# A two-layer language-model tower on one core: four-bit rounding in one step fewer, an output bias added by GpSimd, two small products in different row halves

## The reference, cut to what matters

```python
def step(state, inp):                     # the recurrence, 128 steps, all sequences at once
    d_t, p_t = inp
    state = silu(d_t + state) + p_t
    return (state, state)
h = h + (states @ out_w.T + out_b)        # out_w: (256, 64), out_b: (256,)

def fp4_quant_dequant(x):                 # blocks of 16 along the last dimension
    scale = maximum(max(abs(xb)) / 6.0, 1e-12)
    xn = xb / scale
    idx = searchsorted(_MID, abs(xn))     # nearest of 0, .5, 1, 1.5, 2, 3, 4, 6; ties go down
    return _GRID[idx] * sign(xn) * scale

gate, y = fp4_linear(x, w_gate), fp4_linear(x, w_up)     # 256 -> 704 each
return fp4_linear(silu(gate) * y, w_down)                # 704 -> 256
```

## Time and profile before

| | us |
|---|---|
| median of three runs | 592.85 |
| profiled execution | 593.54 |
| its span, first to last instruction | 591.5 |
| PE busy | 526.8 (89%) |
| DVE busy | 447.4 (76%) |
| ACT busy | 247.7 (42%) |
| POOL busy | 203.6 (34%) |
| mean granted clock of TensorE | 0.958 of full |

### The profile page before, as it was taken

The page is one execution under the profiler, slowest core; times in us unless marked ns, Lnnn a source line. Parts: engine busy times, 40 slices in busy tenths (PEclk is TensorE's granted clock), DMA queues, the critical chain, the costliest instruction groups (busy, mean ns, idle before and its releaser), DMA issues.

```text
span 591.5 us, 9139 instructions
## 1 busy us (share of the span) xinstructions
PE 526.8 (89%) x2919; PEld 317.7 (54%) x2934; DVE 447.4 (76%) x1122; ACT 247.7 (42%) x765; POOL 203.6 (34%) x421
## 2 busy tenths in 40 slices
PE   2789989989999999999998997984569999999994
PEld 1566557456556556555555644632236555565663
DVE  1254788898798789789789787485679998988863
ACT  1174255146246236226317417413345555454431
POOL 6402243233323123113113203120346766775311
PEclk9999999999999999999999998995579999999997
DMA  6800000000000000000000000004200000000000
GB/s 183 277 11 11 9 1 21 9 0 9 18 0 9 9 0 0 0 1 0 0 0 0 0 0 2 1 1 84 58 2 9 20 9 18 10 19 11 18 19 18
DMA packets 13518, 12.76 MB, mean 22 GB/s; under 512 B 2795, under 2 KB 12724, under 8 KB 13492
## 3 DMA queue, kind: packets, MB, share of 16 engines
q1 hardware_dynamic: 12212, 10.34, 6.6%
q0 software_dynamic: 1280, 2.11, 1.3%
HBM read 8.25 MB, written 2.10 MB: 17 GB/s over the span
## 4 chain that ended last, share of the span: by engine, by line
PE 54%; DVE 12%; issue 10%; POOL 9%; ACT 8%; SPq 4%; DMA 2%; DVEq 0%; POOLq 0%; ACTq 0%
PE psum L673 19%; PE psum L627 5%; SPq L392 4%; PE psum L640 3%; DVE neg_max L1350 3%; POOL u_now L528 3%; POOL hq L509 3%; PE psum L755 3%; PE psum L775 3%; PE psum L591 3%; PE psum L739 3%; ACT probs L1036 2%; PE psum L948 2%; PE psum L978 2%; PE psum L964 2%
## 5 line engine op out<-in xcount | busy, mean ns | idle before, releaser
L673 PE MATMUL psum<-expw_sb,n2T 128*128 128x512 f32 x256 | 116.5, 597 | 0.0
L446 POOL TENSOR_TENSOR rstd<-meanvar,ln_eps_col 128x1 f32<-128x1 f32 x64 | 12.7, 199 | 257.4 <-DVE meanvar L1331 257.2
L948 PE MATMUL psum<-wguT,n2T 128*128 128x512 f32 (+1 forms) x192 | 81.7, 576 | 0.0
L1036 ACT ACTIVATE probs<-psum,neg_max 128x128 f32<-128x128 f32 x256 | 69.1, 418 | 27.7 <-DVE neg_max L1350 27.7
L673 PEld LDWEIGHTS psum<-expw_sb,n2T 128*128 128x128 f32 x256 | 46.2, 190 | 45.9 <-issue 45.9
L1004 ACT ACTIVATE probsT<-psum 128x512 f32<-128x512 f32 (+2 forms) x88 | 39.6, 463 | 49.4 <-PE psum L627 30.7
L948 PEld LDWEIGHTS psum<-wguT,n2T 128*128 128x128 f32 x192 | 37.7, 198 | 38.8 <-issue 33.6
L978 PE MATMUL psum<-wdT,probsT 128*128 128x256 f32 x192 | 49.8, 402 | 0.1
L1416 DVE SCALAR_TENSOR_TENSOR acc<-psum,g_w,acc 128x256 f32<-128x256 f32 x96 | 42.1, 479 | 7.5 <-PE psum L673 3.1
L1183 ACT ACTIVATE probs<-u_now 64x16 f32<-64x16 f32 x128 | 27.4, 214 | 47.4 <-POOL u_now L528 31.8
L1350 DVE TENSOR_REDUCE neg_max<-psum 128x4 f32<-128x512 f32 x64 | 40.3, 679 | 6.0 <-PE psum L617 3.8
(11 more groups left out here) (172 smaller groups left out, 980.2 us busy)
## 6 DMA issues: line engine op xcount, KB each, us to landing
expw_sb<-in_expert_w SPq DMA_DIRECT2D x8, 256.0 KB
expw_sb<-hidden SPq DMA_DIRECT2D x16, 128.0 KB
result<-res SPq DMA_DIRECT2D x16, 128.0 KB
w_raw<-in_w_down SPq DMA_DIRECT2D x1, 704.0 KB, 9.1
w_raw<-in_w_gate SPq DMA_DIRECT2D x1, 640.0 KB, 7.2
w_raw<-in_w_up SPq DMA_DIRECT2D x1, 640.0 KB, 7.6
wexp_sb<-in_w_expand SPq DMA_DIRECT2D x1, 256.0 KB, 3.2
wproj_sb<-in_w_project SPq DMA_DIRECT2D x1, 256.0 KB, 3.3
```

Of the source, the lines that this page charges most:

```text
L673: last = mm(pq[:, g, :], n2T[:, u, k, :], expw_sb[:, k, EPQ * g:EPQ * (g + 1), :].rearrange("p e n -> p (e n)"), start=(k == 0), stop=(k = ...
L948: last = mm(pgu[u][:, c0:c1], xqT[:, u, k, :], wguT[:, k, c0:c1], start=(k == 0), stop=(k == KD - 1))
L1036: last = nc.scalar.activation(probs[:, u, h, :], pq[:, g, j * T:(j + 1) * T], ACT.Exp, bias=neg_max[:, u, h:h + 1])
```

## The change

Three edits in one.

**Rounding.** The multiplication of the scale (step 2) goes. The reciprocal is taken of the scale itself, and step 4 becomes one operation with two multiplications, by a factor just under 1 and by the reciprocal. The steps are renumbered: 2 reciprocal, 3 values, 4 ScalarE's sizes, 5 and 6 the rounding. The same is done for the weights (nine steps in place of ten). In DVE's queue step 5 of tile `j + 3` of x (before: step 6 of tile `j + 2`, behind `h_fp4(2, j)`) now stands behind `result(j - 1)`, just ahead of `h_product(j + 1)`.

```diff
                 elif k == 2:
-                    V.tensor_scalar(sc[:, 0, :], sc[:, 1, :], -TIE_DOWN, None, ALU.mult).then_inc(steps[2], 1)
+                    V.reciprocal(sc[:, 0, :], sc[:, 1, :]).then_inc(steps[2], 1)
                 elif k == 3:
-                    V.reciprocal(sc[:, 2, :], sc[:, 0, :]).then_inc(steps[3], 1)
-                elif k == 4:
-                    V.tensor_tensor(t3, s3, per_block(2), ALU.mult).then_inc(steps[4], 1)
+                    V.scalar_tensor_tensor(out=t3, in0=s3, scalar=-TIE_DOWN, in1=per_block(0), op0=ALU.mult,
+                                           op1=ALU.mult).then_inc(steps[3], 1)
...
                 h_fp4(0, j)
                 h_fp4(1, j)
+                if j == 0:
+                    x_fp4(5, j + 2)
                 h_fp4(2, j)
                 if second:
                     x_fp4(6, j + 2)
                 h_fp4(3, j)
-                if second:
-                    x_fp4(7, j + 2)
-                h_fp4(4, j)
                 if third:
                     x_fp4(0, j + 3)
                     x_fp4(1, j + 3)
                     x_fp4(2, j + 3)
                     x_fp4(3, j + 3)
-                    x_fp4(4, j + 3)
                 if fourth:
                     add_outp(j + 4)
+                h_fp4(5, j)
                 h_fp4(6, j)
-                h_fp4(7, j)
...
                 if j > 0:
                     result(j - 1)
+                if third:
+                    x_fp4(5, j + 3)
                 h_product(j + 1, FIRST if j + 2 == TILES else WHOLE)
             j = TILES - 1
-            for k in range(5):
+            for k in range(4):
                 h_fp4(k, j, FIRST)
             h_product(j, SECOND)
             h_fp4(0, j, SECOND)
+            h_fp4(5, j, FIRST)
             h_fp4(6, j, FIRST)
-            h_fp4(7, j, FIRST)
-            for k in range(1, 5):
+            for k in range(1, 4):
                 h_fp4(k, j, SECOND)
             result(j - 1)
+            h_fp4(5, j, SECOND)
             h_fp4(6, j, SECOND)
-            h_fp4(7, j, SECOND)
             result(j)
```

```diff
+            def out_bias(s0, s1):
+                pool.wait_ge(a_rest, 16 * (len(a_loads) - ATTENTION_LOADS))
+                pool.wait_ge(ln_norm[2], s1)
+                pool.tensor_tensor(hidden[:, s0:s1, :], hidden[:, s0:s1, :],
+                                   outb_sb[:].unsqueeze(1).to_broadcast([T, s1 - s0, D]),
+                                   ALU.add).then_inc(out_biased, s1 - s0)
...
                 if rec:
                     rstd_of(2, 1, before)
                     convolved(i, 1, 0, 2)
+                    out_bias(2 * i - 2, 2 * i)
                 gather_amid(i)
...
                     if not front:
                         convolved(i, 0, 0, 1)
                         rstd_of(2, 1, n[1])
+                        out_bias(2 * i, 2 * i + 1)
+                        out_bias(2 * i + 1, 2 * i + 2)
...
-            sp.wait_ge(h3_done, SEQS)
+            sp.wait_ge(out_biased, SEQS)
```

**Row halves.** The last chunk of the 704 rows is taken as the 128 columns 576 to 703, all transposed; the product uses partitions 64 to 127 of it (rows 640 to 703). `outp` uses partitions 0 to 63.

```diff
+HIDDEN_CHUNKS = [(128 * k, 0) for k in range(KI - 1)] + [(INNER - 128, 64)]
...
-                    last = mm(pdown, hqT[0:rows, u, k, :], wdT[0:rows, k, :],
-                              start=(k == 0), stop=(k == KI - 1))
+                    last = mm(pdown, hqT[row:, u, k, :], wdT[row:, k, :], start=(k == 0), stop=(k == KI - 1))
```

More of the change, by code:

```diff
@@ L65 @@
 WEIGHT_PIECES = 6
-WEIGHT_STEPS = 10
+WEIGHT_STEPS = 9
 GU_JOBS = (GU_TILES + 1) // 2
@@ L256, in tower @@
         mix_step = sems("mix_step", 2)
-        h3_done = sem("h3_done")
+        h3_done, out_biased = sem("h3_done"), sem("out_biased")
         xn3T_done, n3T_ready = sem("xn3T_done"), sem("n3T_ready")
@@ L957, in h_transposed @@
                 u, start = j % 2, first_chunks(j)
-                pe.wait_ge(qh[8], j + 1)
-                for k in range(KI):
-                    rows = min(128, INNER - 128 * k)
+                pe.wait_ge(qh[7], j + 1)
+                for k, (c0, _) in enumerate(HIDDEN_CHUNKS):
                     if k == start and j == TILES - 1:
-                        pe.wait_ge(qh[8], j + 2)
+                        pe.wait_ge(qh[7], j + 2)
                     at = k * 128 if k < start else 512 + (k - start) * 128
-                    last = nc.tensor.transpose(pgu[u][0:rows, at:at + 128], hq[:, u, k * 128:k * 128 + rows], ident[:])
+                    last = nc.tensor.transpose(pgu[u][:, at:at + 128], hq[:, u, c0:c0 + 128], ident[:])
                     if k == start - 1:
@@ L971, in down @@
                 wait(pe, res_ready, j)
-                for k in range(KI):
-                    rows = min(128, INNER - 128 * k)
+                for k, (_, row) in enumerate(HIDDEN_CHUNKS):
                     if k == 0:
@@ L1189, in sizes @@
             def sizes(values, dst, steps, n):
-                act.wait_ge(steps[4], n)
-                nc.scalar.activation(dst, values, ACT.Abs, scale=MAGIC).then_inc(steps[5], 1)
+                act.wait_ge(steps[3], n)
+                nc.scalar.activation(dst, values, ACT.Abs, scale=MAGIC).then_inc(steps[4], 1)
             def x_sizes(j):
@@ L1207, in h_transposed @@
                 u = j % 2
-                start, rows = first_chunks(j), INNER - 128 * (KI - 1)
+                start, (_, row) = first_chunks(j), HIDDEN_CHUNKS[KI - 1]
                 act.wait_ge(hqT_done[0], j + 1)
@@ L1215, in h_transposed @@
                 at = 512 + (KI - 1 - start) * 128
-                copy(hqT[0:rows, u, KI - 1, :], pgu[u][0:rows, at:at + 128], hqT_ready[1])
+                copy(hqT[row:, u, KI - 1, :], pgu[u][row:, at:at + 128], hqT_ready[1])
             def x_norm(j):
@@ L1548, in body @@
                     weights(3)
-                    weights(4)
                 if front:
@@ L1670, in _ @@
             x_norm(1)
-            for k in range(5):
+            for k in range(4):
                 x_fp4(k, 1)
                 advance(24 + k)
+            advance(28)
             add_outp(2)
             advance(29)
-            x_fp4(6, 1)
+            x_fp4(5, 1)
             x_stats(2)
             advance(30)
-            x_fp4(7, 1)
+            x_fp4(6, 1)
             x_aggregate(2)
@@ L1683, in _ @@
             x_norm(2)
-            for k in range(5):
+            for k in range(4):
                 x_fp4(k, 2)
-                if k < 4:
-                    advance(33 + k)
+                advance(33 + k)
             h_product(0)
```

94 lines of the change are left out of this document (46 added, 48 removed).

## The result

The changed kernel is slower: 597.76 us (median of eight runs, 595.44 to 599.77) against 593.02 for the kernel before on the same chip (eight runs, 591.31 to 594.3). The ratio is 1.0089, 95% interval 1.0069 to 1.0109 (the two medians alone give 1.0080). The prediction was 591.7 us with a range of 588.9 to 594.8, so even the range missed it.

A forecast was written before the change was run, and what follows sets the result against it. Three nearly equal circles (TensorE, DVE, ScalarE with POOL) were taken to bound the tile loop. +3.4 - 0.95 - 2.6 - 0.3 - 0.7 = -1.15 us, from the median 592.85, forecast 591.7 us, range 588.9 to 594.8.

The forecast's parts named there:

- the sum of the tile loop: Nine full tiles: each falls from 9.50 to 9.22 us, -2.6 us in all (bounds 0 and -4.5).
- The third circle: Tile loop: transposes, ScalarE copies, `x_norm`, five recurrence steps, `h_sizes`, DVE steps, `hq`; 8.9 to 9.3 us, deciding the tile.
- Rival 1: Tile loop not shorter, 9.4 to 9.5 us from DVE collisions; 595.4 (median 594.7), loss above 9.34 a tile; chance 0.2.
- Output bias: Bias add on POOL at the last pair starts the turn's DMAs late, all counted: +3.4 us (3.0 to 3.8).
- In the pair loop: Seven POOL bias additions of 512 columns, about 1.05 us each, covered by other work: 0.
- Merged step: The two-multiplication rounding step costs about what the old multiply did: 0, bounds -0.02 and +0.07 us each.
- Head: Start of the tile loop, 424.5 to 452 us: one rounding step fewer gives -0.95 us (-0.5 to -1.3).
- TensorE's own tile: Tile loop before the change: TensorE's own work, without its waits, is about 9.3 us a tile.
- Row halves: Tile loop: last chunk and `outp` overlap in different row halves, taking 0.2 us off TensorE's circle (0 to 0.43).
- Last tiles: Last five tiles, TensorE-bound, with one `outp` left to overlap: -0.3 us (0 to -0.5).
- Tail: Last half tile: without L1293, slowed to 0.83 us beside POOL's L509, 0.7 us is gained.
- The end: Last product, partly at the lower clock: about 1 us either way by chance, not in the sum.

The follow-up runs named there:

- e5: Kernel before with only the last hidden chunk in rows 64 to 127 and the output product on 64 rows, output bias not computed; 593.46 us.
- e4: Kernel before with the merged rounding step alone, bias row, last chunk and every order as before; 590.15 us.
- e1: Changed kernel with the moved rounding add back between the second and third h steps of the tile loop; 595.39 us.
- e9: Changed kernel with two DVE instructions exchanged: the subtract of x tile j+2 stands behind the hidden's merged step; 595.48 us.
- e3: Changed kernel with the moved add back in its old place and the output bias left out, so the turning DMAs wait only for h3; 591.79 us.
- e2: Changed kernel with the output bias left out of the computation, so the turning DMAs wait only for h3; 594.90 us.

## Why the prediction was wrong

**The step that failed** is the sum of the tile loop: "so the third decides: 8.9 to 9.3", with 0.1 added, "and take 9.22. Nine tiles x (9.50 - 9.22) = -2.6". The third circle was rightly named and wrongly priced: its part from the first transpose to the end of `h_sizes` was taken as 5.59 to 5.93 us plus 0.1 and measured 6.53. Two terms and two assumptions are in it:
- It starts with ScalarE's copies. The text put the 128-row transposes "off the chain: 0" and priced no copy. The copy into rows 64 to 127 puts `x_norm` 0.29 us later (e5).
- The block by DVE was counted as 0.1. It is no average. Both partners return at fixed times after `hq`, so the same step is hit in every tile. In the kernel before the collisions alternated (9.43 and 9.57 in turn), in the changed one they lock on the worst place, 0.95 us for a step of 0.21. From `x_norm` to `h_sizes` this is 3.70 us, against 3.06 to 3.52 in the tiles before, and `h_sizes` ends 6.5 us behind L976 where I expected 5.7 to 6.0.
- DVE's chain of scale steps, shortened by 0.64, was not on this circle: `h_sizes` stands behind five recurrence steps in ScalarE's queue and started 1.5 us after the data was ready in e4. Shortening the chain could only move the collision.
- The moved add L1299 was to fill "a hole of 0.5 in which DVE waited for TensorE", at 0.42 us. It met `hq` and took 0.95, and `h_product` came 0.61 us later after `hq` than with the add in its old place (e1). The merged step came 0.32 later and met the second recurrence step from its first moment; moved 0.16 ahead by an exchange, it held that step less (e9).

What each part does to the tile, by the runs: merged step alone 9.44 (e4), with the halves 9.58 (e3), with the moved add 9.90 (e2). The moved add is the largest part. No run has it without the halves, so whether it would cost as much there stays open.

The Trainium skill (SBUF — State Buffer, Who interferes with whom) has a DVE instruction with two SBUF inputs and a GpSimd one that reads SBUF exclude each other for a whole instruction. Every row here agrees: 0.21 became 0.63, 0.81, 0.84, 0.95 or 0.96, each time until 0.07 to 0.09 us behind the end of the DVE step. I quoted its warning and then gave it 0.1 us.

**Rival 1 is what happened, in kind.** "DVE's operations meet other recurrence steps." Its price, 9.4 to 9.5 us a tile and 594.7, was too low, because the moved add and the copy were missing in it too. Its chance was 0.2. Its break-even of 9.34 us a tile fits the kernels with the late start, which all lose (9.85, e1 9.60, e9 9.57), but none of them comes near it.

The other steps:
- *Output bias, +3.4:* right. 3.5 in the trace, 2.9 (e2) and 3.6 (e1 to e3) in the medians. *In the pair loop, 0:* right, though an addition of 512 columns took 1.27 us and not 1.05; pairs one to seven take the same time in every kernel.
- *Merged step, 0:* right, 882 ns at 704 columns where the multiply took 895.
- *Head, -0.95:* 0.1 in the changed kernel; 0.6 in e4. The first full tile takes 9.89 instead of 9.22 and eats it.
- *TensorE's own tile, "about 9.3":* 9.22. The idle time that the profile shows leaned on modelled ends.
- *Row halves, 0.2 on TensorE:* 0.43 a tile, which was my upper bound. Worth nothing while another circle binds.
- *Last tiles, -0.3:* -0.7, beyond the bound of -0.5: the halves give 0.4 there (e5), and the merged step, which I had left out, 0.3 (e4). *Tail, -0.7:* -0.7, though not where I said: a 0.83 us step remains, on the merged step.
- *The end, "about 1 us either way":* +0.8.

With the loop's +2.9 in place of -2.6 and the head's 0.1 in place of 0.95 the same sum gives +3.4 - 0.1 + 2.9 - 0.3 - 0.7 = 5.2, and 592.85 + 5.2 = 598.05; measured 597.76. That it comes so close is in part luck: the last five tiles gave 1.4 and not 1.0, and start and end, which are not in the sum, brought -1.5 and +0.8. The stretches as measured add up to 4.3.

## What to carry to other kernels

When several circles have nearly one length, follow the one that you shorten least, engine by engine, and price every instruction in it, copies too. A collision of two engines in a periodic loop is a phase and not an average: work out at what time after a common event each partner starts, before and after the edit, and try one exchange of neighbours; here (e9) it was worth 2.3 us, as much as the merged step alone (e4). A new wait in front of a long row of transfers costs its whole delay, so first look for a place where its input is ready earlier.

## What the runs showed of the hardware

- Two float32 products with 64 rows each, in different halves of the array, interleave pass by pass: starts at 496.93 and 496.94, then 497.25 and 497.26. The stretch shrinks from 1.48 to 0.94 us, TensorE's own tile from 9.22 to 8.79. The Trainium skill (TensorE: Matmul & The Clock Gate, Part 3, The mechanism) has matmuls start and end strictly in program order; by the order of the instructions both passes of the chunk come first, and in the kernel before, with 64 and 65 rows, they also ran in that order; yet here the output product's first pass starts before the chunk's second. The measurement decides.
- A ScalarE copy from and into rows 64 to 127 overlaps neither the instruction ahead of it nor the one behind: 0.29 and 0.29 us between starts, against 0.16 and 0.15 with rows 0 to 63, at a duration of 0.27 and 0.26. One copy of 128 rows and 256 columns in place of two brought `x_norm` from 2.11 to 1.78 us after `hq`. Why the rows matter to ScalarE was not tested.
- `h_product`, which reads PSUM and SBUF, runs beside GpSimd's `hq` with almost no effect: 0.89 and 1.39 us in e1, where it starts 0.4 us before `hq` ends; 0.87 and 1.39 in the changed kernel, where it starts 0.2 us after that end.
